# Row sums of the far cells on a third load queue, with landing slots of their own

## What is computed

```python
h     = maximum(layernorm(x), 0)
A_hat = adj + eye(8192)
d     = sum(A_hat, axis=1) ** -0.5
out   = x + relu((d[:, None] * A_hat * d[None, :]) @ (h @ W.T))
```

## Time and profile before

| | us |
|---|---|
| median of 3 runs | 1205.56 |
| lowest and highest | 1199.01, 1219.19 |
| the profiled execution: its span, first to last instruction | 1237.8 |
| PE busy | 983.2 (79%) |
| DVE busy | 802.4 (65%) |
| ACT busy | 586.5 (47%) |
| POOL busy | 52.6 (4%) |

### The profile page before, as it was taken

How to read it: one execution, slowest core, us unless ns; L and a number is a source line. 1 busy time by engine, 2 the same in 40 slices (tenths; PEclk the granted TensorE clock), 3 DMA queues, 4 the chain that set the end, 5 groups by cost and what they waited for, 6 DMA issues and landing times.

```text
span 1237.8 us, 9242 instructions
## 1 busy us (share of the span) xinstructions
PE 983.2 (79%) x2365; PEld 451.8 (36%) x2365; DVE 802.4 (65%) x965; ACT 586.5 (47%) x1735; POOL 52.6 (4%) x61
## 2 busy tenths in 40 slices
PE   0633346566687788796597999999999999899997
PEld 0631122222233333342243444444444444344443
DVE  5342233444476566575485888888888888778775
ACT  2797587776384637145254451724715653010011
POOL 3000000000000000000000000000000000010001
PEclk9767668678889899998798999999999999999999
DMA  9989999999999999999999999999999997999993
GB/s 301 380 320 309 392 398 362 365 369 347 362 349 343 362 337 322 314 256 274 281 291 278 329 332 360 323 276 333 309 325 320 314 271 215 271 271 348 337 328 88
DMA packets 275204, 391.81 MB, mean 317 GB/s; under 512 B 10832, under 2 KB 252624, under 8 KB 275152
## 3 DMA queue, kind: packets, MB, share of 16 engines
q1 hardware_dynamic: 137648, 195.65, 51.3%
q10 hardware_dynamic: 137504, 195.58, 50.5%
...
## 4 chain that ended last, share of the span: by engine, by line
PE 37%; DMA 8%; ACT 6%; ACTq 3%; DVE 1%; issue 0%; POOLq 0%; SPq 0%; DVEq 0%
PE bank L485 36%; DMA slot<-in_adj_dram 8%; ACT junk L540 6%; ACTq L269 2%; DVE adjT L692 1%; ACTq L277 1%; PE pre L461 0%; ACTq L315 0%; DVE near L778 0%; ACT slot L530 0%; ACT near L558 0%; DVE part L677 0%; POOLq L175 0%; PE sums_bank L449 0%; ACTq L321 0%
## 5 line engine op out<-in xcount | busy, mean ns | idle before, releaser
L485 PE MATMUL bank<-adjT,support 128*128 128x512 f32 x2048 | 936.2, 618 | 152.1 <-DVE adjT L692 150.8
L692 DVE STREAM_TRANSPOSE adjT<-slot 128x1024 f32<-128x1024 f32 x450 | 546.5, 1233 | 268.8 <-DMA slot<-in_adj_dram 157.2
L485 PEld LDWEIGHTS bank<-adjT,support 128*128 128x128 f32 x2048 | 401.8, 199 | 664.6 <-issue 661.0
L540 ACT ACTIVATE junk<-slot 128x384 bf16<-128x384 f32 (+2 forms) x540 | 254.6, 473 | 196.1 <-issue 131.3
L530 ACT ACTIVATE slot<-slot 128x6144 f32<-128x6144 f32 (+11 forms) x64 | 191.8, 2998 | 250.3 <-issue 147.8
L558 ACT ACTIVATE near<-near,dinv 128x128 f32<-128x128 f32 x64 | 20.4, 390 | 177.9 <-issue 88.5
L540 ACT ACTIVATION_READ_ACCUMULATOR junk<-slot 128x1 f32 x540 | 100.8, 187 | 0.0
L692 DVE STREAM_TRANSPOSE adjT<-near 128x1024 f32<-128x1024 f32 x62 | 74.8, 1231 | 19.0 <-PE bank L485 19.0
L540 ACT ACTIVATE junk<-near 128x256 bf16<-128x256 f32 (+1 forms) x192 | 75.5, 394 | 2.8 <-ACT junk L540 2.8
L677 DVE TENSOR_REDUCE part<-slot 128x4 f32<-128x1536 f32 (+2 forms) x45 | 69.0, 1533 | 0.0
L407 POOL TENSOR_TENSOR dinv<-total,power 128x4 f32<-128x4 f32 x16 | 16.1, 1007 | 942.0 <-DVE total L746 942.0
...
## 6 DMA issues: line engine op xcount, KB each, us to landing
slot<-in_adj_dram SPq DMA_DIRECT2D x118, 768.0 KB, 15.4
slot<-in_adj_dram ACTq DMA_DIRECT2D x118, 768.0 KB, 13.4
...
near<-in_adj_dram SPq DMA_DIRECT2D x30, 512.0 KB, 16.8
...
```

Source lines behind the costliest of these rows:

```text
L485: ins = nc.tensor.matmul(bank[bank_of(g)][:], support[:, v * R + t, :], adjT[at % TURNS][:, r, :], start=(n == first_of[g] and t == 0), st ...
L540: nc.scalar.activation(junk[at % JUNKS][:, :n], cells[:, c, :], ACT.Copy, accum_out=part[u % 2][:, k, c:c + 1]).then_inc(junk_done, 1)
L692: nc.vector.transpose(adjT[at % TURNS][:].rearrange("p t (c i) -> p t c i", i=Q), half.rearrange("p c (t r) -> p t c r", r=Q)).then_inc(t_ ...
```

## The change

The far cells leave the list `landing`. They are cut in `chunks` of at most 16 runs of 512 B per partition (8 KB): one row block part and one quarter of the columns for 9 to 14 cells a row (16 chunks a stripe), two quarters for 5 to 8 cells (8 chunks), four quarters below. POOL's queue loads them (`load_far`) into three slots of their own (`far_slot`), each when the chunk three before it has been summed. ACT sums most chunks of stripe s + 1 between the left pieces of stripe s, and the last three behind the kept cells of stripe s (`far_share`). The slots of the other pieces become three and `AHEAD` two. The kept cells of stripe s are loaded when its first or second left piece has been summed, no more with the last piece of the loads of the stripe. Small things go with it: POOL makes the four masks ahead of the statistics in four tiles, the far sums have three buffers, and their parts are added by one reduction a stripe.

```diff
     CELL = N // B // NB
     BAND = 1
     MOST = 3
-    SLOTS = 4
-    AHEAD = 3
+    SLOTS = 3
+    AHEAD = 2
+    FAR_SLOTS = 3
+    FAR_RUNS = 16
+    FAR_SUMS = 3
...
-                landing.append(("again", i, u - MOST, MOST, 0, 0))
+                landing.append(("again", i, u - MOST, MOST))
                 next_cell[i] = u
     AGAIN = len(landing)
     for u in AGAIN_ROWS:
         again[u] = []
         for v, n in split(next_cell[u], NB):
             again[u].append(len(landing))
-            landing.append(("again", u, v, n, 0, 0))
+            landing.append(("again", u, v, n))
+
+
+    chunks, far, far_parts = [], {}, {}
+    for u in range(NB):
+        cells = NB - 1 - u - BAND
+        far[u] = []
+        if cells > 0:
+            quarters = 4 if 4 * cells <= FAR_RUNS else 2 if 2 * cells <= FAR_RUNS else 1
+            rows = min(B, FAR_RUNS // (quarters * cells)) if quarters == B else 1
+            rows = 4 if rows >= 4 else 2 if rows >= 2 else 1
+            far_parts[u] = B // quarters
+            for bb in range(0, B, rows):
+                for b in range(0, B, quarters):
+                    far[u].append(len(chunks))
+                    chunks.append((u, bb, rows, b, quarters))
+
+    far_landed = [16 * sum(chunks[k][2] for k in range(i % FAR_SLOTS, i + 1, FAR_SLOTS)) for i in range(len(chunks))]
+
+    def far_share(s, k):
+
+        of, n = far.get(s + 1, []), len(left[s])
+        ahead = max(0, len(of) - FAR_SLOTS) if n else 0
+        return of[ahead:] if k == n else of[ahead * k // n:ahead * (k + 1) // n]
+
+
+    far_before = []
+    for s in range(NB):
+        far_before.append(sum(len(far[k]) for k in range(s + 1)) + sum(len(far_share(s, k)) for k in range(len(left[s]))))
 
     slot_of = [m % SLOTS for m in range(len(landing))]
     before_in_slot, landed = [], []
     for m in range(len(landing)):
         earlier = [k for k in range(m) if slot_of[k] == slot_of[m]]
         before_in_slot.append(earlier[-1] if earlier else None)
-        landed.append(16 * sum(2 * landing[k][3] if landing[k][0] == "far" else B for k in earlier + [m]))
-    by_act = [sum(landing[k][0] != "again" for k in range(m + 1)) for m in range(len(landing))]
-    by_dve = [sum(landing[k][0] == "left" for k in range(m + 1)) for m in range(len(landing))]
...
-        act_freed, dve_freed = sem("act_freed"), sem("dve_freed")
+        act_freed, dve_freed, far_freed = sem("act_freed"), sem("dve_freed"), sem("far_freed")
+        ld_far = [sem(f"ld_far{i}") for i in range(FAR_SLOTS)]
...
-        def load_far(queue, quarters, m):
-            kind, u, bb, n, v, cells = landing[m]
-            to = far_block(m).rearrange("p a (b j) -> p a b j", b=B)
-            b0 = quarters[0]
-            for a in range(n):
-                queue.dma_start(to[:, a, b0:b0 + 2, :],
-                                adj_far[u, :, bb + a, b0:b0 + 2, v * CELL:(v + cells) * CELL]
-                                ).then_inc(ld_slot[slot_of[m]], 16)
...
-                queue.wait_ge(act_freed, by_act[before])
-                if landing[before][0] == "left":
-                    queue.wait_ge(dve_freed, by_dve[before])
+                queue.wait_ge(act_freed, lefts_by[before])
+                queue.wait_ge(dve_freed, lefts_by[before])
-            if landing[m][0] == "far":
-                load_far(queue, quarters, m)
-            else:
-                load_cells(queue, quarters, m)
+            load_cells(queue, quarters, m)
...
-        last_piece = {(far[u] + left[u])[-1]: u for u in range(NB)}
+        kept_with = {left[u][min(1, len(left[u]) - 1) if column_at[u - 1] > stripe_at[u] else 0]: u for u in range(2, NB)}
...
+            for u in range(2):
+                load_kept(sp, (0, 1), u)
             for m in range(AGAIN):
                 load_piece(sp, (0, 1), m)
-                if m in last_piece:
-                    load_kept(sp, (0, 1), last_piece[m])
+                if m - AHEAD in kept_with:
+                    load_kept(sp, (0, 1), kept_with[m - AHEAD])
...
+            def load_far(i):
+                u, bb, rows, b, quarters = chunks[i]
+                if i >= FAR_SLOTS:
+                    pool.wait_ge(far_freed, i - FAR_SLOTS + 1)
+                to = far_block(i).rearrange("p a (b j) -> p a b j", b=quarters)
+                for a in range(rows):
+                    nc.gpsimd.dma_start(to[:, a, :, :], adj_far[u, :, bb + a, b:b + quarters, (u + BAND + 1) * CELL:]
+                                        ).then_inc(ld_far[i % FAR_SLOTS], 16)
+
+            for i in range(FAR_SLOTS):
+                load_far(i)
             nc.gpsimd.memset(ident[:], 0.0).then_inc(ident_ok, 1)
             nc.gpsimd.memset(power[:], -0.5).then_inc(ident_ok, 1)
             nc.gpsimd.memset(far_of[:], 0.0).then_inc(ident_ok, 1)
...
-            ones_where([[-Q // R, R], [-Q, B], [-1, Q // R]], 2)
-            ones_where([[-1, R], [-Q, B], [-R, Q // R]], 3)
+                while issued < min(len(far[0]), FAR_SLOTS + (q + 1) * TX // R):
+                    load_far(issued)
+                    issued += 1
...
             def root(u):
                 pool.wait_ge(total_ok, u + 1)
                 nc.gpsimd.tensor_tensor(dinv[:, u * R:(u + 1) * R], total[:], power[:, :R], ALU.pow).then_inc(root_ok, 1)
 
             for u in range(NB):
+                while issued < min(far_before[u] + FAR_SLOTS, len(chunks)):
+                    load_far(issued)
+                    issued += 1
                 root(u)
...
             def next_piece(m):
 
                 load_piece(act, (2, 3), m + AHEAD)
-                if m + AHEAD in last_piece:
-                    load_kept(act, (2, 3), last_piece[m + AHEAD])
-
-            def far_sums(m):
-                u = landing[m][1]
-                act.wait_ge(ld_slot[slot_of[m]], landed[m])
-                next_piece(m)
-                for a in range(landing[m][3]):
-                    at = landing[m][2] + a + (B if landing[m][4] > u + BAND + 1 else 0)
-                    ins = nc.scalar.activation(far_block(m)[:, a, :], far_block(m)[:, a, :], ACT.Copy,
-                                               accum_out=far_sum[u % 2][:, at:at + 1])
-                ins.then_inc(act_freed, 1)
+
+            def far_sums(i):
+                u, bb, rows, b, quarters = chunks[i]
+                act.wait_ge(ld_far[i % FAR_SLOTS], far_landed[i])
+                for a in range(rows):
+                    part_of = b // quarters
+                    ins = nc.scalar.activation(far_block(i)[:, a, :], far_block(i)[:, a, :], ACT.Copy,
+                                               accum_out=far_sum[u % FAR_SUMS][:, bb + a, part_of:part_of + 1])
+                ins.then_inc(far_freed, 1)
...
+            for u in range(2):
+                load_kept(act, (2, 3), u)
...
                     for b in range(NB):
+                        far_sums(far[0][b])
                         layernorm(b)
-                        if b % 4 == 3:
-                            far_sums(far[0][b // 4])
-                    for m in far[0][NB // 4:]:
-                        far_sums(m)
-                else:
-                    for m in far[s]:
-                        far_sums(m)
                 for k, m in enumerate(left[s]):
                     left_sums(m, k, summed)
                     summed += 1
+                    if m in kept_with:
+                        load_kept(act, (2, 3), s)
+                    for i in far_share(s, k):
+                        far_sums(i)
                 act.wait_ge(ld_near[s % 2], 16 * B * (s // 2 + 1))
                 late_sums(near[s % 2][:, :, :min(2, NB - s) * CELL], s, len(left[s]), summed)
                 summed += 1
                 act.wait_ge(junk_done, summed * (C - DVE_C))
                 act.sem_inc(act_sums, 1)
+                for i in far_share(s, len(left[s])):
+                    far_sums(i)
                 if s >= BAND + 1:
...
-                if far[u] and landing[far[u][-1]][4] > u + BAND + 1:
-                    nc.vector.tensor_tensor(far_sum[u % 2][:, :B], far_sum[u % 2][:, :B], far_sum[u % 2][:, B:],
-                                            ALU.add).then_inc(both_far, 1)
+                if far[u]:
+                    nc.vector.tensor_reduce(far_total[:], far_sum[u % FAR_SUMS][:, :, :far_parts[u]], AX.X, ALU.add).then_inc(both_far, 1)
                     dve.wait_ge(both_far, u + 1)
-                if far[u]:
-                    nc.vector.tensor_tensor(far_by_block[:], far_sum[u % 2][:, :B].unsqueeze(1).to_broadcast([P, R, B]),
+                    nc.vector.tensor_tensor(far_by_block[:], far_total[:].unsqueeze(1).to_broadcast([P, R, B]),
```

54 lines of the change are left out of this document (26 added, 28 removed).

## The result

The changed kernel takes 1304.2 us (1300.4 to 1307.1) against 1203.8: a ratio of 1.084, 95% interval 1.081 to 1.088. The forecast was 1205, its range ended at 1248. Its profiled span is 1301.6 us, near its own median. That of the kernel before was some 32 us over its median, so against that profile only 64 of the 100 us are to be seen.

What follows compares the result with a forecast made beforehand. Loads were taken to bound the kernel up to about the total of row block 10, PE after it. Terms 3 - 14 + 4 + 6 = -1 us gave 1205 us against the median, no change; 8-in-10 range 1155 to 1248.

Steps and rivals of the forecast that it cites:

- the ring of far chunks: Stripes 1 to 4: three chunks circulate with a trip of 6.3 us, 376 GB/s; +4 us, bounds 0 to +16.
- What bounds: Whole kernel: loads set the pace up to about the total of row block 10, PE after it.
- Start: Before total 0: three early chunks delay loads of `x` by up to 6.6 us; taken as 0, +7 for the range.
- A stripe ahead: Next stripe's far chunks before each total: 28 us later in stripe 1, but only +3 us at row block 10.
- Rate while loads bound: Mainly 507 to 684 us: a third queue beside left pieces eases the queues' turns; -14 us, between -32 and 0.
- ACT and POOL: Mostly stripes 0 to 5: 24 us more ACT sums stay covered and POOL's scales do not wait; 0 each.
- Three slots: One landing slot less: 0 while loads bound, cost from 684 us on and behind the stripes; +6 us, bounds 0 to +21.
- A: Rival, faster: the third queue keeps both partition halves busy, 340 GB/s or more from 500 us; 1159 us, chance 0.30.
- B: Rival, slower: with three slots, stretches of turns reach PE after 684 us, DVE waits for slots; 1243 us, chance 0.12.
- C: Rival, slower: mixed far and left cells run at 282 GB/s in half of 92 to 507 us; 1259 us, chance 0.10.
- E: Rival: POOL issues chunks slowly or waits for slots, making scales and chunks late in 14 stripes; 1233 us, chance 0.04.
- D: Rival: all queues share full engines, so the rate stays and slots, ring and order cost +13; 1218 us, chance 0.14.

Runs made afterwards that it cites:

- a_start: The changed kernel with layer norm before the first pieces' issues on ACT and variances before far chunks on GpSimd: 1299.6 us, ratio 1.080.
- c_all: The changed kernel with four far buffers of 14 runs, the unblocked start and a fourth landing slot behind the stripes: 1253.1 us, ratio 1.040.
- c_ahead_from_2: c_all with the far chunks of stripe 2 loaded in stripe 2, a stripe ahead only from stripe 3 on: 1254.6 us, ratio 1.038.
- b_same_half: The kernel before with SyncE loading partition quarters 0 and 2 and ScalarE 1 and 3, not 0, 1 and 2, 3: 1598.8 us, ratio 1.328.
- b_three_slots: The kernel before with three landing slots instead of four and pieces issued two ahead instead of three: 1264.1 us, ratio 1.048.
- b_packed: The kernel before with its four landing slots as one room of 192 runs, pieces packed by their own size: 1224.2 us, ratio 1.017.
- a_far_on_sp: The changed kernel with the far chunks issued by SyncE between its pieces instead of by GpSimd: 1368.2 us, ratio 1.135.
- a_late_slot: The changed kernel with the far buffers' memory as a fourth landing slot behind the stripes: 1292.5 us, ratio 1.074.
- a_four_chunks: The changed kernel with four far buffers of 14 runs instead of three of 16, ACT's scrap output moved to PSUM: 1277.1 us, ratio 1.059.
- c_not_ahead: c_all with the far chunks of stripes 1 to 9 loaded in their own stripe, not a stripe ahead: 1301.9 us, ratio 1.080.

## Why the prediction was wrong

The main step that failed is the ring of far chunks, +4 us: its trip of 6.3 us was 8.0, and the share of the DMA engines fell from 0.97 to 1.04 down to 0.91 to 0.94 up to total 4. Around it stood two more: that a rate can only stay or rise (-14), and that a slot less costs nothing while loads bound (0). For total 10 the sum of the prediction had about -7 us against the profile; it came 37 us later. Step by step, as it put them:

- **What bounds.** Right: loads up to total 10 and PE after it. PE was without gaps from about 804 us to the last total at 1082.5.
- **Start, 0 (+7).** Wrong: total 0 came 10.1 us late, over the 7 that it named as its limit. I looked at what three chunks do to the loads of `x`, and not at ACT, whose queue took eight issues in 15.24 us (8.57 before) and then eight more in 19.4. a_start gave 4.4 us of it back.
- **A stripe ahead, +3.** The sizes fit: the 28 us that it gave to stripe 1 were 31 in c_all (total 1 at 166.8 us, 135.3 in c_ahead_from_2), and they made no difference at total 10. But its effect on the order of loads was missed: without it the changed kernel is 70 us slower.
- **Rate while loads bound, -14.** Wrong in two ways. The reading of the slow stretch is right, as b_same_half shows. But its length was very likely an accident of the one profiled run, 26 of the 32 us that I then took off again: b_three_slots and b_packed go through it at 323 and 333 GB/s, and of their slices of 2 us 9 and 7 in 75 are under 240 GB/s, of the profile's 25 in 88. Against the median there was little to win: the term and the correction counted the same time twice. And I let the rate only stay or rise; it fell, as the next item shows.
- **The ring, +4 (0 to +16).** A fourth chunk gave 27 us, two chunks cost 65. The trip was put together from a landing of 64 KB and a peak rate, as if each chunk were alone. So it was nearly right for a ring of two (6.6 us), not for three: these chunks took 6.2 to 8.8 us to land, and 6.0 to 8.2 on SyncE's queue. 11.19 MB in 35 us are 320 GB/s, not 376, and packets were slower too. The 8.0 us lie just beyond the 7.8 (1.5 us more a trip) from which the +16 came. The share of 0.91 and 0.94 is just over the mark of 0.9 that I had set for this failure, so the mark was too low: 1.04 stood there before.
- **ACT and POOL, 0.** ACT's sums and a chunk's landing follow each other in the ring, so its waits, and not its busy time, are on the path: 124 us for far chunks. GpSimd's issue takes 0.53 us, each scale began within 0.1 us of its total, and a_far_on_sp frees its queue of blame. For POOL the 0 was right.
- **Three slots, +6 (0 to +21).** 12 to 14 us behind the stripes (a_late_slot), within the bounds. With the slot back 6 of the 20.6 us are left: PE waits 7.6 us for DVE there (14.0 in the changed kernel, 4.6 before) and is busy 2.6 us longer than before. In front I took 0 "while loads bound". In the kernel before the same cut cost about 29 us there. For the changed kernel that part couldn't be measured, since a fourth slot doesn't fit beside the far buffers.

The rivals. A did not come: 335 and 327 GB/s from total 4 to 10, where it asked for 340. B asked for waits of DVE for slots. It had them right, but behind the stripes, not in them: of these 25.8 us from total 10 on, in the changed kernel, 8.4 lie before total 15 (PE waited 6.5 us there), against 20.6 us lost behind it. Its price of 37 us is not reached.

```profile
DVE adjT L722 <- DMA slot<-in_adj_dram: 25.8, 7, 8.4
PE bank L516 <- DVE adjT L722: 20.5, 7, 7.1
```

C has its mark (296 GB/s from 189.6 to 349.7 us), but hardly its mechanism. For a share of 1 the window of 60 to 350 us gives 343 GB/s in a_four_chunks and 338 in c_all, where far and left cells mix, 344 in c_not_ahead, where they mix least (313 at 0.91), and 351 in the kernel before (358 at 1.02). Mixing costs at most some 4%; what cost more was the missing share, 0.90 to 0.94. E is wrong: scales were never late, and it was ACT's sums that freed the next chunk last. D, that spreading over a third queue gains nothing, is true as far as it goes. The rule of the Trainium skill that it named ("DMA: Bandwidth & Descriptors", rules for kernel authors: issuing loads from one more engine brings no bandwidth) agrees with every run here: the best kernel with a third queue took 1253.1 us against 1203.8. D had no word for the loss.

Two of the prediction's sums slipped. The upper end of its likeliest case, with the rate at 0 and the ring at 16, is 1231 us and not 1228, and C's 1259 leaves out the 13 us of the other terms that A and D have. Neither changes what failed.

What stays open is c_all's 49 us. Its total 10 is 40 to 46 us behind that of a usual run before (698.2 against 652 to 658), its DMA shares of 0.99 and 1.01 stand against 1.02 and 1.05 in the same windows of the kernel before, and early bytes are not the cause. The likely one is the third slot, which cost the kernel before 29 us in this part. That is argued, not shown.
